# Two transformer layers on one core: where the turned heads of the first attention pass from TensorE to their SBUF tile

## What is computed

```python
x = L0_attn_hidden_states
xn = _layernorm(x, axis=-1)
x = x + _L0_attn_ref(xn, ...) + _L0_ffn_ref(xn, ...)
xn = _layernorm(x, axis=-1)
x = x + _L1_attn_ref(xn, ...) + _L1_ffn_ref(xn, ...)
return x

# in _L0_attn_ref
scores = jnp.einsum('bhncd,bhnkd->bhnck', qb, kb) / scale
scores = jnp.where(valid[None, None], scores, -jnp.inf)
p = jax.nn.softmax(scores, axis=-1)
o = jnp.einsum('bhnck,bhnkd->bhncd', p, vb)
o = o.reshape(B, H, T, D).transpose(0, 2, 1, 3).reshape(B, T, E)
return o @ wo + bo
```

## Time and profile before

| | |
|---|---|
| runs of the kernel | 1351.73 us median of 3 (1345.3, 1351.73, 1352.2) |
| the profiled execution | 1352.31 us, its span 1350.3 us |
| granted TensorE clock, mean over the span | 0.956 |
| PE busy in the span | 1197.0 us (89%) |
| DVE busy | 896.5 us (66%) |
| ACT busy | 673.1 us (50%) |
| one loop element of phase A | 57.60 us |

### The profile page before, as it was taken

The page is one execution under the profiler, slowest core; times in us unless marked ns, Lnnn a source line. Parts: engine busy times, 40 slices in busy tenths (PEclk is TensorE's granted clock), DMA queues, the critical chain, the costliest instruction groups (busy, mean ns, idle before and its releaser), DMA issues.

```text
span 1350.3 us, 27031 instructions
## 1 busy us (share of the span) xinstructions
PE 1197.0 (89%) x8812; PEld 814.6 (60%) x8812; DVE 896.5 (66%) x2474; ACT 673.1 (50%) x1294; POOL 466.9 (35%) x695
## 2 busy tenths in 40 slices
PE   4999999999999966983799898998989889899896
PEld 2656656666666636882566657666566665666654
DVE  6988988888888836553456557566575655655644
ACT  2766676666766632541452643525435354353540
POOL 4221222222122136551352542534425344252340
PEclk8999999999999976996799899999999989999999
DMA  2300100100100025230000000000000000000000
GB/s 74 91 18 17 24 17 17 24 17 16 25 17 17 17 65 162 62 58 20 1 9 1 16 0 8 8 0 15 1 8 8 0 12 4 3 13 0 8 2 8
DMA packets 34597, 29.78 MB, mean 22 GB/s; under 512 B 5984, under 2 KB 27104, under 8 KB 34528
## 3 DMA queue, kind: packets, MB, share of 16 engines
q1 hardware_dynamic: 32224, 24.22, 6.6%
q0 software_dynamic: 2304, 4.72, 1.7%
HBM read 13.72 MB, written 6.82 MB: 15 GB/s over the span
## 4 chain that ended last, share of the span: by engine, by line
PE 38%; issue 12%; ACT 5%; POOL 5%; DVE 3%; DMA 3%; POOLq 1%; ACTq 0%; DVEq 0%
PE ring_a L465 15%; PE ring_d L465 13%; PE gather L465 7%; ACT arena L1400 3%; DMA arena<-tokens_x,tokens_now 2%; PE ring_a L469 2%; ACT xn_all L1380 1%; POOL arena L1116 1%; POOL v_aug L1057 1%; POOL q_len L1163 1%; DVE arena L1916 0%; DVE k_rows L1844 0%; ACT k_rows L1339 0%; ACT arena L1372 0%; POOL klen L1169 0%
## 5 line engine op out<-in xcount | busy, mean ns | idle before, releaser
L1255 ACT ACTIVATE arena<-ring_a 128x384 f32<-128x384 f32 (+1 forms) x512 | 252.5, 550 | 139.1 <-PE ring_a L465 139.0
L1400 ACT ACTIVATE arena<-ring_a 128x896 f32<-128x896 f32 (+1 forms) x192 | 163.3, 885 | 206.7 <-PE ring_a L465 206.7
L1531 DVE CUSTOM_DVE_ANT_0 arena<-ring_d,arena 128x512 bf16<-128x512 f32 (+1 forms) x391 | 231.4, 614 | 38.0 <-PE ring_d L465 31.8
L1027 POOL TENSOR_SCALAR_AFFINE_SELECT arena<-arena 128x512 f32<-128x512 f32 x128 | 81.5, 637 | 357.4 <-ACT arena L1255 357.4
L465 PE MATMUL ring_a<-rows,k_rows 64*128 64x512 f32 (+3 forms) x1536 | 160.4, 342 | 43.8 <-ACT xn_all L1380 26.4
L465 PE MATMUL ring_a<-q_max,rows 128*128 128x384 f32 (+1 forms) x512 | 195.5, 385 | 0.9 <-ACT arena L1255 0.5
L465 PEld LDWEIGHTS ring_a<-rows,k_rows 64*128 64x128 f32 x1536 | 120.8, 192 | 81.4 <-ACT xn_all L1380 29.3
L1163 POOL TENSOR_TENSOR q_len<-q_sum,exponents 128x8 f32<-128x8 f32 x64 | 105.2, 1644 | 182.3 <-DVE q_sum L1820 182.3
L465 PE MATMUL ring_d<-rows,q_rows 128*128 128x512 f32 (+1 forms) x391 | 161.2, 414 | 6.1 <-DVE mx L1531 3.3
L465 PE MATMUL ring_d<-arena,v_aug 128*64 128x512 f32 (+3 forms) x1024 | 150.2, 438 | 0.0
L465 PE MATMUL ring_a<-arena,v_aug 128*32 128x384 f32 (+1 forms) x1024 | 122.8, 551 | 1.9 <-POOL arena L1027 1.0
(11 more groups left out here) (226 smaller groups left out, 1983.8 us busy)
## 6 DMA issues: line engine op xcount, KB each, us to landing
rows<-k_rows SPq DMA_DIRECT2D x128, 64.0 KB, 2.0
arena<-in_w SPq DMA_DIRECT2D x2, 2048.0 KB, 14.1
slots_y<-arena SPq DMA_DIRECT2D x40, 64.0 KB, 1.6
x_all<-in_x SPq DMA_DIRECT2D x8, 256.0 KB, 3.8
tokens_x<-xn_all SPq DMA_DIRECT2D x1, 2048.0 KB, 9.6
out<-o_t SPq DMA_DIRECT2D x8, 256.0 KB, 2.3
arena<-tokens_x,tokens_now POOLq DMA_INDIRECT x40, 2.9
wq_sb<-in_wq_t SPq DMA_DIRECT2D x1, 512.0 KB, 4.8
```

The lines of the kernel that those rows point to most:

```text
L1027: pool.affine_select(out=v, in_=v, compare_op=ALU.is_ge, fill=0.0, base=0, pattern=[[0, HG], [1 if late else -1, P]], channel_multiplier=- ...
L1255: act.activation(probs[:, t % NT, h, 0:many], A.slot(("cols", c))[:, 0:many], ACT.Exp).then_inc(A.free.sem, A.free.add(1))
L1400: act.activation(dst, src, ACT.Exp).then_inc(A.free.sem, A.free.add(1))
L1531: dve.tensor_tensor_reduce(dump[:, h % 2, 0:many], M.slot(("max", n))[:, 0:many], masks[:, m, at:at + many], 1.0, LOWEST, ALU.add, ALU.max ...
```

## The change

Bank `gather` moves from ring M to ring A: M has three banks and A four halves or banks. The turned heads are a fill of A where they were one of M, and ACT copies them to `o_t` where DVE did; ACT's copy stands in its program at step 36, ahead of the exponential of that step. `project_out` waits for A's release of it. The counts of fills follow (75 of M and 76 of A in a loop body).

```diff
-PER_A = dict(m_full=(1, 71, 76, 75, 5), m_free=(1, 71, 76, 75, 5), a_full=(5, 54, 75, 70, 21), a_free=(5, 54, 75, 70, 21),
+PER_A = dict(m_full=(1, 71, 75, 74, 4), m_free=(1, 71, 75, 74, 4), a_full=(5, 54, 76, 71, 22), a_free=(5, 54, 76, 71, 22),
...
-        M = Fills(now, SA["m_full"], SA["m_free"], [bank[:] for bank in banks_d] + [gather[:]])
-        A = Fills(now, SA["a_full"], SA["a_free"], [banks_a[0][:, 0:T], banks_a[0][:, T:2 * T], banks_a[1][:, 0:T]])
+        M = Fills(now, SA["m_full"], SA["m_free"], [bank[:] for bank in banks_d])
+        A = Fills(now, SA["a_full"], SA["a_free"], [banks_a[0][:, 0:T], banks_a[0][:, T:2 * T], banks_a[1][:, 0:T], gather[:]])
...
             def turn_heads():
 
                 at_least(pe, M.free, M.emptied(("o.T", G - 1)))
-                at_least(pe, M.free, M.fillable("heads.T"))
-                turn(M.slot("heads.T"), lambda i: o_n[:, i, :]).then_inc(M.full.sem, M.full.add(1))
+                at_least(pe, A.free, A.fillable("heads.T"))
+                turn(A.slot("heads.T"), lambda i: o_n[:, i, :]).then_inc(A.full.sem, A.full.add(1))
 
             def project_out():
 
-                at_least(pe, M.free, M.emptied("heads.T"))
+                at_least(pe, A.free, A.emptied("heads.T"))
...
+            def heads_turned():
+
+                at_least(act, A.full, A.filled("heads.T"))
+                act.activation(o_t[:], A.slot("heads.T"), ACT.Copy).then_inc(A.free.sem, A.free.add(1))
...
             def attend():
 
                 for n in range(FINISH if now.kind == "finish" else SLOTS):
+                    if n == now.heads and now.past:
+                        heads_turned()
                     if now.own if n >= COLS_LAG else now.past:
                         exp_of((n - COLS_LAG) % SLOTS)
...
-            def heads_turned():
-
-                at_least(dve, M.full, M.filled("heads.T"))
-                dve.tensor_copy(o_t[:], M.slot("heads.T")).then_inc(M.free.sem, M.free.add(1))
...
-                    if n == now.heads and now.past:
-                        heads_turned()
```

## The result

The changed kernel takes 1360.79 us (median of 16 runs, 1353.26 to 1364.51); the kernel before, in 16 runs beside it, 1349.61 us (1344.18 to 1355.86). The ratio is 1.0082, 95% interval 1.0064 to 1.0101: the change makes the kernel 11 us slower. Forecast were 9.8 us and 0.7%. All ratios here leave out slow runs, of which there were two (one of e10 at 1891.84 us, one of the kernel before beside e11 at 6347.28 us).

What follows compares the result with a forecast made beforehand. PE's own instruction stream was taken to bound most of an element. The terms 0.48 + 0.15 + 0.48 + 0.21 - 0.1 = 1.22 us, times 8, gave 9.8 us on 1351.73, so 1361.5 us; 8-in-10 range 1353 to 1369.

Steps and rivals of the forecast that it cites:

- the four places: Steps 63 to 5, 13, 17 and 35 to 37 of a loop element, where the third fill back is released too late.
- the fill of 277.29: Fill of M in steps 35 to 37, at 277.29 us before the change, expected to be held 0.63 us late.
- first place: Steps 63 to 5: fills of M wait for DVE's releases, up to 1.20 us late, and 0.48 us remains.
- step 13: The fill at 258.12 waits for a release at 258.09; 0.15 us remains, and DVE waits for PE soon after.
- step 17: The fill at 261.28 waits for a division ending at 261.59; 0.48 us remains, with no later wait to swallow it.
- the heads' place: Steps 35 to 37: the turned heads no longer wait for M, so 0.21 us remains in place of 0.63.
- ring A: Ring A going from three to four returns between nothing and 0.43 us an element; 0.1 was taken.
- First and last element: Fewer delays last in the first, one more late place in the last; both taken as ordinary, 1.22 us each.
- A sign that did not come: DVE's busy time in a loop element would be down by 0.68 us.
- A: Rival: PE catches up at two late places, leaving 0.53 us an element, 4.2 us in all, 1355.9 us; chance 0.23.
- B: Rival: DVE releases later after each late fill, so 2.46 us an element remains, 19.7 in all, 1371.4 us; chance 0.12.
- C: Rival: DVE is the bound, so its lost copy and ring A's waits save 8.3 us, 1343.4 us; chance 0.07.

Runs made afterwards that it cites:

- e10: Kernel before with only the turned heads passed through ring A and copied by ACT, a second run of that change: element 57.37 us, ratio 0.9989.
- e11: Kernel before with only the routing of the next element moved from steps 58-63 to 42-50: element 57.03 us, ratio 0.9980.
- e4_small_copy: Kernel before with DVE's copy of the turned heads cut from 512 to 8 columns: element 57.60 us, ratio 0.9992.
- e1_three_banks: Kernel before with only the fourth bank of ring M taken away, ring A and the heads unchanged: element 59.41 us, ratio 1.0115.
- e3: Kernel before with three banks in M and four in A, the turned heads still in M and copied by DVE: element 59.31 us, ratio 1.0092.

## Why the prediction was right, and where its terms were off

*The bound.* Right. PE's own stream bounds an element and DVE's total does not: 0.53 us less work on DVE was worth 0.02 us (e4_small_copy). The reading of start distances, and not of busy shares, decided it. The rule that the prediction quotes from the Trainium skill (Perfetto Trace Analysis, Identifying the Most-Contended Engine), by which DVE would have been the engine to relieve, would have led to 1343 us.

*The mechanism.* Right: fills of M are held to about 0.06 us behind the release of the third fill back, and the delays merge within a place. The bank alone accounts for more than the whole loss (e1_three_banks). Three of the four places are those foreseen. At the fourth the wrong fill was named: the hold is at step 33, behind a division, and the fill of 277.29 is not held. The Trainium skill (Perfetto Trace Analysis, Optimization Strategy) says that a gap that repeats on the engine that should be saturated can mean too little SBUF or PSUM for the next tile; e1 against before shows that here for PSUM, with 1.8 us in every element.

*The terms of one element*, forecast and measured (the lateness of PE's starts against before, place by place): first place 0.48, measured 0.83; step 13 0.15, measured 0.02; step 17 0.48, measured 0.45; the heads' place 0.21, measured 0.17; ring A -0.1, measured -0.09. The measured ones add up to 1.38, and small shifts of 0.03 make it 1.41 against 1.22.

- The first place was too small because its releases were taken from the trace of before as they stood. The 0.43 us by which PE came late moved ACT's exponentials and POOL's selection by as much, and the selection ran into a DVE write that it had just missed. DVE lost 0.31 us, PE the same behind it. This is the term of the sum that was most in error.
- Step 13 was too large: the fill was 0.13 us late there, but the `values` group behind it started only 0.02 late. In front of this group PE's stream had about 0.1 us of its own to lose ("issue" in the brackets of the weight loads: 0.34 before, 0.25 after), which the small hold used up. At step 17 the same bracket reads 0.24 in both kernels, and nothing was swallowed.
- The heads' place came out near its 0.21 us by luck in part. Its hold was taken as 0.63 us at the fill of 277.29. In its place 0.48 us arise at steps 31 to 34, which were not walked, and the heads' move gives 0.31 of them back, not 0.42.

*First and last element.* Both were taken as ordinary, 1.2 us each. The first lost 3.2, the last and the finish together 0.7. The step that failed is the sentence that DVE is the bound in the first element, so that fewer delays last. Stretches of the first element, before and after:

```profile
22.70:73.50 50.80, 48.53 (x239) 31.01 (x239) 45.05 (x158) 29.22 (x59) 9.79 (x14) 0.92 0.35 95
```

```profile
23.20:77.20 54.00, 49.94 (x239) 30.03 (x239) 45.97 (x161) 29.27 (x59) 9.81 (x14) 0.97 0.34 89
```

DVE has 5.7 us of 50.8 to spare there and 8 us after: neither engine is the bound throughout. In all kernels with three banks in M the first element took 54.0 to 54.6 us, in all with four 50.4 to 51.8, at clocks from 0.86 to 1.00, so the 3.2 us are the bank's. A likely account is that PE and DVE take turns there and the ring carries the one past the other's bursts; which fills were late in the first element was not read. In the last stretch ring A's fourth half returned about 1 us (e3 against e1).

*The sum.* 13.2 us in phase A for 9.8 forecast; by the runs 11.2 us (8.6 to 13.6) for 9.8. That the time, 1360.79, lies only 0.7 us under the 1361.5 is luck: the loss was 1.4 us larger than forecast, and the kernel before came out 2.1 us lower in 16 runs than in the three of the prediction.

*A sign that did not come.* DVE's busy time was to fall by 0.68 us an element. It fell by 0.17 in the element shown. The busy time counts overlapping records of DVE once; added up one by one they fell by 0.8 to 1.0 us in two elements compared, 0.68 of it the copy and 0.4 the long writes.

*The rivals.* A (PE catches up) did not happen: both places ended later than before. B (the delays add) came nearer at the first place, where 0.83 us lie between the forecast's 0.48 and B's 1.20, but for the reason given above and not for the one that it named. C fell.

## What to carry to other kernels

How many slots a ring needs is read slot by slot, as the time between the release of a slot and the start of its next fill: the places where that is shorter than one release interval are the price of giving one up. The list repeats from element to element, but it has to be walked whole: three of DVE's four divisions in an element were such a place here, and the prediction passed one over. A ring between two busy engines can look spare on average and still need its last slot where the consumer has extra work. Moving that work to steps where the consumer is ahead shortened the element with four banks (57.37 to 56.57 us) and with three (59.03 to 58.34), but did not make up for the bank. Taking a copy off an engine that is soon idle anyway was worth 0.02 us (e4_small_copy); what the heads' move saved was PE's hold.

## What the runs showed of the hardware that was not expected

*A small DVE write that begins inside a selection of POOL ends with it.* A DVE write of 128x16 takes 0.18 or 0.19 us. The 15 long ones before and the 8 after, 0.39 to 0.57 us, all began 0.1 to 0.3 us into a selection of 128x512 and ended 0.03 to 0.04 us behind that selection's end. It matters which comes first: 14 writes of the changed kernel began about 0.01 us ahead of a selection and took 0.19 us in spite of 0.18 us of overlap. The selections behind them took 0.68 us, where 0.64 is usual. One such pair:

```profile
271.02 0.19 DVE L1546 SCALAR_TENSOR_TENSOR m_cols<-mx,m_cols 128x16 f32<-128x16 f32 x1
271.03 0.68 POOL L1027 TENSOR_SCALAR_AFFINE_SELECT arena<-arena 128x512 f32<-128x512 f32 x1 [2.03 <-ACT arena L1260]
```

With the selection cut to 8 columns a head all 64 writes of each kernel stay under 0.2 us. The long custom instructions on DVE (0.56 us) showed no such effect beside the same selections. In most elements the kernel before has two such long writes and the changed one only one, but that one stands where PE waits for it.

*The scatter of the runs goes with the granted clock, most of it in phase C.* One element of phase C, three in a row in the kernel before, two in the changed one:

```profile
744.20:831.90 87.70, 80.24 (x672) 55.72 (x672) 52.51 (x114) 38.61 (x60) 35.52 (x53) 0.96 0.02 6
831.90:918.50 86.60, 78.89 (x672) 54.49 (x672) 52.56 (x114) 38.49 (x60) 35.51 (x53) 0.98 0.02 6
918.50:1003.70 85.20, 77.34 (x672) 53.25 (x672) 52.61 (x114) 38.24 (x60) 35.34 (x53) 1.00 0.02 6
```

```profile
755.60:840.80 85.20, 77.31 (x672) 53.27 (x672) 52.62 (x114) 38.25 (x60) 35.41 (x53) 1.00 0.02 6
840.80:926.00 85.20, 77.29 (x672) 53.21 (x672) 52.62 (x114) 38.29 (x60) 35.43 (x53) 1.00 0.02 6
```

The same instructions take 85.2, 86.6 or 87.7 us as the granted clock averages 1.00, 0.98 or 0.96. From line 1655 to the end the profiled execution of the changed kernel takes 843.7 us and that of the kernel before 853.0; 7.7 of these 9.3 us lie in seven elements of phase C (595.2 against 602.9 us, clock 1.00 against 0.98), and they hid two thirds of phase A's loss there. The changed program does nothing else in phase C. The spread of 11 to 12 us between the fastest and the slowest of the 16 runs goes the same way: a lower mean clock over the span goes with a longer time (0.971 and 1353.26 us, 0.960 and 1364.51 us for the changed kernel). What decides where the clock falls was not tried.
